# A fused decoder layer: the weight fold on parts of the array, two steps of x moved into its key part, and another order in the tail

## The reference

```
x = x + scan_attention(layernorm(x))                 # q * scan(sigmoid(a), kv)
x = x + layernorm(out) * ln_scale + ln_bias          # out from the cross attention below
x = x + ffn(layernorm(x))
# cross attention: 16 heads of 64, 64 context rows and one null key and value per batch
q = y @ Wq;  k, v = split(context @ Wkv)             # context 64 x 512 per batch
out = softmax([nk, k] . q / 8) @ [nv, v] @ Wout
# ffn: weights ternary, activations rounded to 127 steps per row
ffn = quant(silu(quant(x) @ wg.T) * (quant(x) @ wu.T)) @ wd.T
```

## Time and profile before

| | |
|---|---|
| median of three runs | 560.01 us |
| the profiled execution | 559.87 us |
| its span | 558.0 us |
| PE busy in the span | 502.2 us (90%) |
| DVE, ACT, POOL busy | 438.0, 332.3, 305.4 us |
| mean granted TensorE clock | 0.976 of 2.4 GHz |

### The profile page before, as it was taken

One profiled execution on the slowest core, in us unless ns is written; L12 is line 12 of the kernel. 1 busy time (PEld: TensorE's weight loads), 2 busy tenths in 40 slices (PEclk: granted clock), 3 DMA queues, 4 the chain that ended last, 5 costly groups with the idle time before them and its releaser, 6 DMA issues.

```text
span 558.0 us, 9285 instructions
## 1 busy us (share of the span) xinstructions
PE 502.2 (90%) x2906; PEld 403.1 (72%) x2906; DVE 438.0 (78%) x959; ACT 332.3 (60%) x450; POOL 305.4 (55%) x483
## 2 busy tenths in 40 slices
PE   2889999998998889999999999999999999998663
PEld 1667787765687788788778778778878878866231
DVE  5899998969634676788888888888888888875673
ACT  4422351432242343678877887888788778776671
POOL 3112325500000267887787777877877877887541
PEclk9999999999999899999999999999999999998786
DMA  8991000000000000002213212312221231222233
GB/s 281 367 396 51 1 0 1 0 2 1 0 1 0 1 2 2 10 6 42 49 34 43 57 35 45 47 44 34 54 49 33 53 40 43 45 46 62 49 81 79
DMA packets 57949, 30.49 MB, mean 55 GB/s; under 512 B 44336, under 2 KB 55856, under 8 KB 57904
## 3 DMA queue, kind: packets, MB, share of 16 engines
q1 hardware_dynamic: 57904, 29.93, 21.0%
HBM read 15.24 MB, written 4.19 MB: 35 GB/s over the span
## 4 chain that ended last, share of the span: by engine, by line
POOL 31%; issue 23%; PE 22%; DVE 17%; DMA 4%; ACT 1%; POOLq 1%; DVEq 1%; ACTq 0%
PE psum L1134 13%; POOL region_d L528 5%; POOL xs L508 3%; POOL region_d L506 3%; POOL region_d L504 3%; PE psum L1150 3%; POOL sc L538 3%; POOL sc L551 3%; DVE region_a L865 3%; PE psum L1375 2%; POOL region_d L562 2%; PE psum L1380 2%; POOL region_d L519 2%; POOL region_c L567 2%; DMA region_d<-region_d 2%
## 5 line engine op out<-in xcount | busy, mean ns | idle before, releaser
L516 POOL TENSOR_TENSOR region_d<-region_d,rden 128x1024 f32<-128x1024 f32 x32 | 60.9, 1902 | 118.2 <-DVE rden L1002 118.2
L1134 PE MATMUL psum<-Mhi,xT2hi 128*128 128x260 f32 x256 | 75.2, 294 | 1.9 <-DVE xT2lo L959 1.6
L1134 PE MATMUL psum<-Mlo,xT2hi 128*128 128x260 f32 x256 | 72.6, 284 | 0.0
L1134 PE MATMUL psum<-Mhi,xT2lo 128*128 128x260 f32 x256 | 72.6, 284 | 0.0
L1375 PE MATMUL psum<-VW,region_d 128*128 128x256 f32 x256 | 62.7, 389 | 4.6 <-DVE pTn L1051 4.6
L1015 DVE SCALAR_TENSOR_TENSOR region_c<-psum,zw,region_c 128x1024 f32<-128x1024 f32 x29 | 37.2, 1283 | 29.8 <-ACT region_c L688 29.8
L1380 PE MATMUL psum<-VW,region_d 128*128 128x256 f32 x256 | 60.5, 379 | 0.0
L1375 PEld LDWEIGHTS psum<-VW,region_d 128*128 128x128 f32 x256 | 49.1, 194 | 15.0 <-DVE pTn L1051 6.0
L1380 PEld LDWEIGHTS psum<-VW,region_d 128*128 128x128 f32 x256 | 48.7, 190 | 6.7
L985 DVE TENSOR_REDUCE mx<-psum 128x8 f32<-128x520 f32 x64 | 44.2, 690 | 8.9 <-PE psum L1134 7.7
L1134 PEld LDWEIGHTS psum<-Mhi,xT2hi 128*128 128x128 f32 x256 | 48.6, 190 | 3.0 <-issue 2.7
(11 more groups left out here) (150 smaller groups left out, 1269.7 us busy)
## 6 DMA issues: line engine op xcount, KB each, us to landing
out_dram<-xs SPq DMA_DIRECT2D x32, 128.0 KB, 1.9
xs<-in_x_dram SPq DMA_DIRECT2D x1, 2560.0 KB, 17.0
VW<-in_L_xattn_Wkv_dram SPq DMA_DIRECT2D x1, 2048.0 KB, 16.8
region_b<-in_L_xattn_Wkv_dram SPq DMA_DIRECT2D x1, 2048.0 KB, 16.8
xs<-in_x_dram SPq DMA_DIRECT2D x3, 512.0 KB, 6.4
region_w<-in_L_ffn_w_gate_dram SPq DMA_DIRECT2D x1, 1024.0 KB, 10.5
region_w<-in_L_ffn_w_up_dram SPq DMA_DIRECT2D x1, 1024.0 KB, 12.9
region_w<-in_L_ffn_w_down_dram SPq DMA_DIRECT2D x1, 1024.0 KB, 16.7
```

Source lines behind the costliest of these rows:

```text
L516: pool.tensor_tensor(p2[:, v, 0:H * MK].rearrange("p (h j) -> p h j", j=MK), e[:, :, 0:MK], rden[:, v, :].unsqueeze(2).broadcast_to([P, H, ...
L1134: mm = pe.matmul(dst, lhsT, rhs, start=i == 0, stop=i == len(terms) - 1)
```

## The change

The fold uses parts of the array instead of a block diagonal operand. `kv_T`'s result is copied as it is into one of four buffers `kvT` by ACT alone (`put_kvT`), and `bd`, its clearing and DVE's half of the copies go. `fold_keys(i)` multiplies rows 0 to 63 and rows 64 to 127 apart (one head each), four matmuls of 64 × 128 over 256 columns, the two heads in different banks. `fold_values(q)` does two pairs at a time in 16 matmuls of 64 × 64 over 256 columns, into the upper or lower 64 partitions of banks 2 to 5; `slot_of` gives the order of heads that follows from it, which the null key and value take on too. Keys: ACT makes both high parts, DVE both rests. Values: two copies each per round of two pairs. The first `norm2_pair`s, `pair_T(0, 0)` and its evictions move into the key half, the second pair's transposes to the first value round. PE's waits ahead of the pipeline shrink to the keys; those for the values stand at the second half of the first scores, that for the null values at its product.

In the tail the down product comes ahead of `gate_up`, `residual` ahead of `hidden_layer`, and the silu table is not loaded from n = 31 on.

```diff
-            pool.memset(f["bd"], 0.0).then_inc(bd_zero, 1)
...
+            def put_kvT(i):
                 act.wait_ge(fT_psum, i + 1)
+                if positive(i - 3):
+                    act.wait_ge(fold_psum, i - 3 if i - 4 < HC else HC + (i - 4 - HC) // 2 + 1)
+                act.activation(kvT[:, i % 4, :], bank(i % 2, BM), ACT.Copy).then_inc(kvT_ready, 1)
+            def put_keys_hi(i):
                 act.wait_ge(fold_psum, i + 1)
+                for half_ in range(2):
+                    at = slot_of(2 * i + half_) * J
+                    act.activation(Mhi[:, :, :, at:at + MK],
+                                   bank(2 + 2 * (i % 2) + half_).rearrange("p (k b j) -> p k b j", k=KD, b=B),
+                                   ACT.Copy).then_inc(m_hi, 1)
+            def put_values_second(q):
+                act.wait_ge(fold_psum, HC + q + 1)
+                for half_ in range(2):
+                    act.activation(VW[:, 2:4, 2 * q + half_, :], bank(3 + 2 * half_).rearrange("p (b n) -> p b n", b=2),
+                                   ACT.Copy).then_inc(vw_second, 1)
...
-                act.preload_act_table(ACT.Silu)
+                if n < T - 1:
+                    act.preload_act_table(ACT.Silu)
...
+            put_kvT(0)
+            for i in range(HC):
+                put_kvT(i + 1)
+                put_keys_hi(i)
+                if i == 5:
+                    act.wait_ge(nmr2_done, NG)
+                    norm2_pair(0, 0)
+                    norm2_pair(1, 1)
+            act.wait_ge(mnull_put, KD)
+            xT2_pair(0, 0)
+            put_kvT(HC + 1)
+            for q in range(HC // 2):
+                for i in (HC + 2 * q + 2, HC + 2 * q + 3):
+                    if i < 2 * HC:
+                        put_kvT(i)
+                put_values_second(q)
+                if q == 0:
                     act.wait_ge(vwn_psum, 1)
                     act.activation(VWnull[:, :], psum[0:NP, 7, 0:D], ACT.Copy).then_inc(vwn_hi, 1)
+                    xT2_pair(1, 1)
...
-                dve.tensor_reduce(mnull[:, k, :], heads, AX.X, ALU.add).then_inc(mnull_done, 1)
+                for odd in range(2):
+                    dve.tensor_reduce(mnull[:, k, :].rearrange("p (a y x) -> p a y x", y=2, x=2)[:, :, odd, :],
+                                      heads.rearrange("p (a x y) d -> p a x y d", x=2, y=2)[:, :, :, odd, :],
+                                      AX.X, ALU.add).then_inc(mnull_done, 1)
...
+            def put_keys_lo(i):
+                for half_ in range(2):
+                    at = slot_of(2 * i + half_) * J
+                    dve.wait_ge(m_hi, 2 * i + half_ + 1)
+                    dve.tensor_tensor(Mlo[:, :, :, at:at + MK],
+                                      bank(2 + 2 * (i % 2) + half_).rearrange("p (k b j) -> p k b j", k=KD, b=B),
+                                      Mhi[:, :, :, at:at + MK].bitcast(F32), ALU.subtract).then_inc(m_lo, 1)
+            def put_values_first(q):
+                dve.wait_ge(fold_psum, HC + q + 1)
+                for half_ in range(2):
+                    dve.tensor_copy(VW[:, 0:2, 2 * q + half_, :], bank(2 + 2 * half_).rearrange("p (b n) -> p b n", b=2)) \
+                        .then_inc(vw_first, 1)
...
+            for i in range(HC):
+                put_keys_lo(i)
                 if i in (2, 4):
                     null_key((i - 2) // 2)
                 if i == 6:
                     null_values()
+            xT2_lesser(0, 0)
+            for q in range(HC // 2):
+                put_values_first(q)
+                if q == 0:
                     dve.wait_ge(vwn_hi, 1)
...
+                if q == 1:
+                    xT2_lesser(1, 1)
...
+                if late(n):
+                    residual(n - 7)
                 if late(n) and exists(n - 5, T):
                     hidden_layer(n, v)
...
-                if late(n):
-                    residual(n - 7)
...
+            def fold_keys(i):
                 pe.wait_ge(wqT0_ready, 1)
                 pe.wait_ge(wqT1_ready, 1)
+                pe.wait_ge(kvT_ready, i + 1)
+                if positive(i - 1):
+                    pe.wait_ge(m_lo, 2 * (i - 1))
+                first = 2 + 2 * (i % 2)
+                for k in range(KD):
+                    for half_ in range(2):
+                        rows = slice(half_ * DH, (half_ + 1) * DH)
+                        mm = pe.matmul(psum[:, first + half_, k * BM:(k + 1) * BM], wqT[rows, i, k * P:(k + 1) * P],
+                                       kvT[rows, i % 4, :], start=True, stop=True)
+                mm.then_inc(fold_psum, 1)
+            def fold_values(q):
                 pe.wait_ge(wout_loaded, 16)
+                pe.wait_ge(kvT_ready, HC + 2 * q + 2)
+                if q == 0:
+                    pe.wait_ge(m_lo, 2 * HC)
                 else:
+                    pe.wait_ge(vw_first, 2 * q)
+                    pe.wait_ge(vw_second, 2 * q)
+                for b in range(B):
+                    for half_ in range(2):
+                        for column in range(2):
+                            rows, pair = slice(half_ * DH, (half_ + 1) * DH), 2 * q + column
+                            mm = pe.matmul(psum[column * MK:(column + 1) * MK, 2 + 2 * half_ + b // 2,
+                                                (b % 2) * D:(b % 2 + 1) * D],
+                                           kvT[rows, pair % 4, b * MK:(b + 1) * MK], wout[rows, pair, :],
+                                           start=True, stop=True)
                 mm.then_inc(fold_psum, 1)
...
+            for i in range(HC):
+                kv_T(i + 1)
+                fold_keys(i)
+                if i == HC - 2:
+                    pe.wait_ge(wdT_ready, 1)
+                    pair_T(0, 0)
+            kv_T(HC + 1)
+            for q in range(HC // 2):
+                if q + 1 < HC // 2:
+                    kv_T(HC + 2 * q + 2)
+                fold_values(q)
+                if q + 1 < HC // 2:
+                    kv_T(HC + 2 * q + 3)
+                if q == 0:
                     pe.wait_ge(nv_set, 2 * HC)
                     group(psum[0:NP, 7, 0:D],
                           [(nvsel[:, pair * NP:(pair + 1) * NP], wout[:, pair, :]) for pair in range(HC)]) \
                         .then_inc(vwn_psum, 1)
+                    pair_T(1, 1)
             def scores_half(n, hh, u4, q, b):
                 pe.wait_ge(xT2_lo_ready, q + 1)
+                if n == 0 and hh == 1:
+                    pe.wait_ge(vw_first, HC)
+                    pe.wait_ge(vw_second, HC)
...
-            pe.wait_ge(vwn_ready, 1)
-            pe.wait_ge(fold_even, 2 * HC)
-            pe.wait_ge(fold_odd, 2 * HC)
+            pe.wait_ge(m_lo, 2 * HC)
             pe.wait_ge(mnull_put, KD)
-            pe.wait_ge(xT2_lo_ready, 2)
...
-                if isinstance(n, int) and n >= T - 1 and exists(n - 4, T):
-                    gate_up(n + 1, u)
                 if exists(n - 7, T):
...
                     group(bank(5, D), [(nhT3[v][:, k, :], wdT[:, k, :]) for k in range(FC)]) \
                         .then_inc(down_psum, 1)
+                if isinstance(n, int) and n >= T - 1 and exists(n - 4, T):
+                    gate_up(n + 1, u)
```

More of the change, by code:

```diff
@@ L257, in decoder_layer @@
         mnull_put = sem("mnull_put")
-        bd_zero = sem("bd_zero")
         nvsel_zero = sem("nvsel_zero")
         fT_psum = sem("fT_psum")
-        bd_upper = sem("bd_upper")
-        bd_lower = sem("bd_lower")
+        kvT_ready = sem("kvT_ready")
         fold_psum = sem("fold_psum")
[L264 to L267, removed]
+        m_hi = sem("m_hi")
+        m_lo = sem("m_lo")
+        vw_first = sem("vw_first")
+        vw_second = sem("vw_second")
         mnull_hi = sem("mnull_hi")
@@ L923, in null_values @@
                         rows = slice(j * DH, (j + 1) * DH)
-                        column = nvsel[rows, :].rearrange("p (c m h) -> p c m h", c=HC, h=H)[:, pair, 0::2, 2 * pair + j]
+                        column = nvsel[rows, :].rearrange("p (c m h) -> p c m h", c=HC, h=H)[:, pair, 0::2, slot_of(2 * pair + j)]
                         dve.tensor_copy(column, nv[rows, :].broadcast_to([DH, 3])).then_inc(nv_set, 1)
[L927 to L953, removed]
+            def put_keys_lo(i):
[5 more added lines that the diff above has]
+                                      Mhi[:, :, :, at:at + MK].bitcast(F32), ALU.subtract).then_inc(m_lo, 1)
@@ L960, in xT2_lesser @@
                                   ALU.subtract).then_inc(xT2_lo_ready, 1)
-            put_bd_lower(0)
-            for i in range(2 * HC):
-                if i + 1 < 2 * HC:
-                    put_bd_lower(i + 1)
-                put_fold_even(i)
+            for i in range(HC):
+                put_keys_lo(i)
                 if i in (2, 4):
@@ L1231, in kv_T @@
                 if positive(i - 1):
[L1232 to L1234 removed]
+                    pe.wait_ge(kvT_ready, i - 1)
```

(30 more changed lines are left out.)

48 lines of the change are left out of this document (7 added, 41 removed).

## The result

The changed kernel takes 543.55 us (median, 541.14 to 544.6) against 559.89 us: a ratio of 0.9707 with a 95% interval of 0.9682 to 0.9731, 16.3 us less. The forecast was 547.7 us, within 543 to 558. The profiled execution after is at 541.14 us, the fastest of its four, so trace against trace the difference is larger (18.9 us of span) than between the medians. The measured time is some 4 us under the forecast and close to the lower end of the range.

The account below looks back on a forecast made before the run. PE was taken to bound the fold, with DVE interrupting it. A fold gain of 11.0 us (63.3 to 52.3) plus 1.3 in the tail made 12.3: 559.87 - 12.3 + 0.14 = 547.7 us, range 543 to 558.

Parts of the forecast that it names:

- The bound: Fold: PE binds it, with DVE interrupting; 57.9 us of PE work and 5.4 us idle in 63.3 us.
- Keys and values: Fold products: row halves overlap, 0.865 us per key call (6.9 us); values limited by issue, 1.9 us per call (7.6 us).
- Rival B: Fold: parts of the array do not overlap in f32; values 27.6 us, kernel 574.6 us; chance 0.08.
- rival C: Fold: weight loads limit; keys 1.34 and values 4.4 us per call, kernel 561.6 us; chance 0.07.
- Rival A: Value folds: only two quarters run at a time, 3.46 us per call, kernel 553.9 us; chance 0.25.
- Changes between full and part array: Fold on PE: 24 changes, 16 around keys and 8 around values, at 0.25 us each, 6.0 us.
- Rival D: Fold: overlap holds but changes cost 0.5 us each, or DVE is late before the values; 554 us; chance 0.15.
- Waits: PE in the fold: old waits go, including 1.58 us before the scores; a new 1.6 us wait at `fold_values(3)`.
- The tail: Tail: dropped table loads give 3.3 us, a loop through DVE takes some back; gain 0.4 to 2.1, taken as 1.3.

Follow-up runs that it names:

- v_same_quarter: Changed kernel with the batch loop innermost in `fold_values`, so one quarter's four matmuls follow each other: value fold 4.70 us, fold stretch 61.06 us.
- values_out_first: Changed kernel with ACT copying a round's values out before the odd `put_kvT`: fold stretch 49.11 us against 50.13.
- tail_only: Kernel before with only the three tail edits (table load, `residual` order, down product order): 556.85 us, ratio 0.9951.
- fold_only: Changed kernel with the three tail edits undone, so new fold and old tail: 546.24 us against 559.94, ratio 0.9767.
- hidden_first: Changed kernel with `residual` back behind `hidden_layer` on DVE: 541.24 us, ratio 0.9663.
- keys_in_twos: Changed kernel with the key half ordered as two `kv_T`, then two `fold_keys`: 541.63 us, fold stretch 49.57 us.
- x_late: Changed kernel with the first two pairs of x back in the value half and the scores waiting for both: fold stretch 52.01 us.
- after_again: The changed kernel itself measured once more: 542.79 us, ratio 0.9696.
- table_only: Kernel before with only the silu table load left out from n = 31 on: 558.58 us, ratio 0.9978.
- all_mended: Changed kernel with key folds in twos, null keys and values moved, values out first, `residual` behind `hidden_layer`: 539.55 us, ratio 0.9627.
- the two alternating orders: Changed kernel with column or row half outermost in `fold_values`, two quarters taking turns: value fold 2.87 us, fold stretch 53.78 us each.

## Why the prediction was right, point by point

*The bound.* PE bound the fold, as the busy time and the waits said. Where PE's work fell, the time fell with it, and DVE did not take over. From the end of the third key fold (121.95 us) its last key split took 18.5 us and PE reached `fold_values(0)` after 19.0; 18.4 and 19.4 were computed. Of the 13.15 us, some 9.4 come from the products (27.6 us of `fold` against 6.9, 6.9 and 4.4 us for keys, values and changes) and the rest from waits, 5.4 us before and 1.54 after.

*Keys and values.* Both row halves at once was right: four pairs of instructions 0.216 us apart, 0.865 us, and 0.2 us around them. Four quarters at once was right too, but the 1.9 us per call that stood in the sum was met by luck. It came from an issue of 0.06 us for every instruction with its load. That limit is not there: four instructions start within 0.02 us. A call is eight groups of 0.216 us, 1.73 us, and the 0.16 us up to the measured 1.89 belong to the changes. Rival B (no overlap) and rival C (loads limit) are out, by 1.06 us per key call and 1.89 per value call. Rival A (two at a time) fell for a reason that the prediction had left open: a second instruction of a quarter does not stop those behind it. The Trainium skill, "TensorE: Matmul & The Clock Gate", Part 3, section The mechanism, says that matmuls start and end in program order. The starts here don't agree: in `v_same_quarter` the next quarter's first instruction starts at 142.50 us, ahead of three earlier ones of the first quarter, the last at 143.14. The measurement decides, and A's 3.5 us per call are refuted by 1.89.

*Changes between full and part array.* This term was too large: 24 of 0.25 us, 6.0 us, were booked. Around the keys a change costs 0.2 us (twos against singles, and 2.99 - 1.73 - 0.865 = 0.39 for two), 3.1 us in all. Around the values it is about as much: 0.16 us of each call and 0.10 us in the `kv_T` behind, which takes 1.83 instead of 1.73; with the `kv_T` before them, some 1.3 us for all. That makes some 4.4 us, 1.6 less than booked, and the values are 0.7 us less (6.9 against 7.6). With 11.0 forecast and 13.15 measured for the fold, these two account for the difference. Rival D (0.5 us a change, or DVE late) is out. The Trainium skill, "TensorEngine Tiling (Array Packing)", Key Properties, has a drain at each change of mode. A loss at each change is in this trace, 0.2 us; whether the array empties in it the trace doesn't tell.

*Waits.* 1.6 us before the last value fold was forecast and 1.54 measured, on ACT as said, and `values_out_first` shortens it to 0.52. The wait of 1.58 us before the scores is gone, as forecast.

*The tail.* Forecast were 0.4 to 2.1 us, and 1.3 was taken. In the medians `tail_only` gives 3.1 us. In the traces it depends on the clock at the last null-value product. With that stretch at 1.2 GHz in both (before and `tail_only`) the tail falls from 42.1 to 40.4 us, 1.8 us; the casts of tile 26, tile 28 and the last one come 0.8, 3.2 and 1.8 us earlier, where 0.7, 3.3 and 2.1 were worked out. With it at full clock in both (`fold_only` and after) the tail falls from 43.6 to 40.0 us, 3.6 us, more than I had. The -2.1 us of the table compares a trace of one kind with one of the other. That the order on DVE costs time is shown by `hidden_first`. What the loads bring alone I had wrong in the runs' expectations: 1.4 us in the medians and not 3.3.

*What the forecast did not have.* The middle, in which nothing was changed, is 3.7 us shorter in the trace of after. The granted clock of the stretches around the first weighted sum and around that of n = 31, before and after:

```profile
186.50:190.00 3.50, 3.42 (x16) 3.40 (x17) 1.68 (x3) 1.82 (x6) 0.03 (x1) 0.51 0.00 0
510.50:514.50 4.00, 3.58 (x9) 2.90 (x10) 0.89 (x3) 3.97 (x6) 3.49 (x7) 0.57 0.19 51
```

```profile
173.50:176.50 3.00, 2.96 (x24) 2.91 (x25) 1.97 (x4) 2.27 (x5) 0.00 (x0) 1.00 0.02 5
495.70:499.20 3.50, 3.43 (x17) 3.05 (x17) 1.70 (x4) 2.70 (x4) 3.07 (x5) 1.00 0.20 56
```

Before, PE runs both for nearly their whole length at 1.2 GHz (0.51 and 0.57), after, both at 2.4. In both kernels the first piece follows a wait of PE of 2.08 and 2.07 us, so the wait alone doesn't decide. `hidden_first`, which is after up to there, has them slow again:

```profile
173.50:177.50 4.00, 3.80 (x19) 3.78 (x20) 1.68 (x3) 2.32 (x6) 0.15 (x1) 0.57 0.00 0
```

Over the profiles the middle takes 335.9 to 336.0 us (after, `fold_only`, `keys_in_twos`, `x_late`), 337.5 to 338.2 (`after_again`, `values_out_first`, `v_same_quarter`, `table_only`) or 339.2 to 339.6 (`hidden_first`, `all_mended`, `tail_only`, the two alternating orders, before). It goes with the execution and not only with the kernel: after and `after_again`, the same kernel, differ by 1.6 us, and `hidden_first`, the same up to there, by 3.3. The first piece costs about 1.6 us and the second 1.8. Of the second, part comes back: with the table loads in place the tail behind it takes 42.1 us (before) against 43.6 (`fold_only`, no slow piece). So the change as such is worth 13.15 us of fold and 1.8 to 3.6 of tail, 15 to 17 us, and the 16.3 us between medians lie in that. Of what came beyond the 12.3 forecast 2.2 us are the fold's, and the rest lies in the tail and in how the slow pieces fell; so the time is near the lower end of the range. Whether slow pieces come less often with the shorter fold stays open: there is one profile of before and two of after.

## What to carry to other kernels

Where a product has a block diagonal operand, ask for parts of the array instead: the same f32 work at half the time, at about 0.2 us per change between full and part. Give the parts in short turns (two instructions here), as a fourth one waiting on a part stops all others. And look at an order of waits on two engines together: leaving out 1.28 us of table load per tile brought 1.4 us alone, and 3.1 us with the down product and `residual` moved ahead as well.

## What the runs showed of the hardware that I had not expected

- Quarters of 64 by 64 overlap fully with f32 operands, 32 instructions in 1.96 us, though the two instructions of a matmul follow each other on one quarter. Four start within 0.02 us.
- The engine hands on instructions past three that wait for their quarter, and stands at the fourth (4.70, 2.87 and 1.96 us for three orders of the same 32). By that, matmuls of different quarters start out of program order.
- A change costs at two places: 0.09 us before the first instruction of the new kind, and 0.05 us (64 by 64) or 0.10 us (64 by 128, and back to full) more than 0.216 us between the first and the next on the same part.
- The middle, in which nothing differs, took 335.9 to 339.4 us in the profiles with the new fold, by two pieces at 1.2 GHz of some 3.5 us each.
